# A two-layer attention and mixture kernel on one core: the contexts of eight heads as one step or as two

## The reference, cut to what matters

```
gate_v = _get_sel_gate(x, sel_v_w, rs)      # top 2 of 8 experts per head
gate_o = _get_sel_gate(x, sel_o_w, rs)
xv  = einsum('bsd,hedp->bshep', x, v_w)     # 64 products of 128x128 per batch
v   = einsum('bshep,bshe->bhsp', xv, gate_v)
att = softmax(einsum('bhqp,bhkp->bhqk', q, k) * SCALE, axis=-1)
ctx = einsum('bhqk,bhkp->bqhp', att, v)     # the contexts
out = einsum('bshep,hepd->bsd', ctx[:, :, :, None, :] * gate_o[..., None], o_w)
```

## Time and profile before

| what | us |
|---|---|
| median of 3 runs | 1510.36 |
| the profiled execution, whole | 1512.08 |
| its span, first to last instruction | 1509.9 |
| PE busy | 1439.0 |
| DVE busy | 1320.1 |
| ACT busy | 1274.5 |
| POOL busy | 861.5 |
| PE idle in the first 160 us | 51.6 |
| mean granted TensorE clock over the span | 0.975 |

### The profile page before, as it was taken

One profiled execution on the slowest core, in us unless ns is written; L12 is line 12 of the kernel. 1 busy time (PEld: TensorE's weight loads), 2 busy tenths in 40 slices (PEclk: granted clock), 3 DMA queues, 4 the chain that ended last, 5 costly groups with the idle time before them and its releaser, 6 DMA issues.

```text
span 1509.9 us, 34239 instructions
## 1 busy us (share of the span) xinstructions
PE 1439.0 (95%) x9905; PEld 971.3 (64%) x9905; DVE 1320.1 (87%) x4496; ACT 1274.5 (84%) x4428; POOL 861.5 (57%) x1345
## 2 busy tenths in 40 slices
PE   3678999999999999999999999999999999999997
PEld 2355666666666666666666666666666666666654
DVE  3767988999999999999999999999999999999886
ACT  3667888899888888988888898888889988888886
POOL 2112666565565656556565665656566565655567
PEclk8588999999999999999999999999999999999999
DMA  4510000000000000000000000000000000000000
GB/s 126 148 46 17 13 16 15 14 13 14 12 14 14 16 14 13 14 12 15 13 16 14 13 14 12 14 14 16 14 13 13 12 16 13 16 11 6 7 3 4
DMA packets 68954, 30.13 MB, mean 20 GB/s; under 512 B 19168, under 2 KB 68768, under 8 KB 68768
## 3 DMA queue, kind: packets, MB, share of 16 engines
q1 hardware_dynamic: 51552, 19.31, 4.8%
q10 hardware_dynamic: 17216, 8.65, 2.0%
HBM read 17.31 MB, written 2.10 MB: 13 GB/s over the span
## 4 chain that ended last, share of the span: by engine, by line
PE 86%; POOL 4%; DVE 4%; issue 2%; ACT 2%; DMA 1%; SPq 1%; POOLq 0%; ACTq 0%; DVEq 0%
PE psC L307 55%; PE psA L307 14%; PE psB L307 7%; PE psB L530 3%; PE psC L626 2%; POOL accO L3426 2%; POOL TE L3414 1%; PE psA L463 1%; PE psB L550 1%; DVE TE L2487 1%; PE psA L419 1%; POOL v_sb L3419 1%; DVE PTB L2350 1%; PE psC L572 1%; DVE nmA L2226 1%
## 5 line engine op out<-in xcount | busy, mean ns | idle before, releaser
L3426 POOL TENSOR_TENSOR accO<-accO,TE 128x512 f32<-128x512 f32 x192 | 246.7, 1285 | 140.8 <-DVE TE L2487 133.9
L2487 DVE SCALAR_TENSOR_TENSOR TE<-psC,gateO,TE 128x128 f32<-128x128 f32 x1024 | 287.5, 343 | 32.5 <-ACT TE L1334 23.6
L1334 ACT ACTIVATE TE<-psC,gate 128x128 f32<-128x128 f32 x1024 | 303.4, 420 | 9.5 <-PE psC L307 8.1
L2487 DVE SCALAR_TENSOR_TENSOR TE<-psC,gate,TE 128x128 f32<-128x128 f32 x1024 | 287.8, 343 | 25.9 <-PE psC L307 19.3
L1334 ACT ACTIVATE TE<-psC,gateO 128x128 f32<-128x128 f32 x1024 | 289.3, 380 | 20.1 <-PE psC L307 11.9
L3414 POOL TENSOR_TENSOR TE<-TE 128x256 f32<-128x256 f32 x256 | 189.3, 739 | 166.0 <-DVE TE L2487 159.5
L307 PE MATMUL psC<-Vh,xTh 128*128 128x512 f32 x512 | 266.1, 520 | 1.9 <-DVE TE L2487 0.6
L307 PE MATMUL psC<-Oh,ch 128*128 128x512 f32 x512 | 266.1, 520 | 1.1 <-DVE cl L2479 0.9
L307 PE MATMUL psC<-Oh,cl 128*128 128x512 f32 x512 | 202.5, 396 | 0.0
L307 PE MATMUL psC<-Vh,xTl 128*128 128x512 f32 x512 | 202.3, 395 | 0.0
L307 PE MATMUL psC<-Vl,xTb 128*128 128x512 bf16 x512 | 199.7, 390 | 0.0
(11 more groups left out here) (226 smaller groups left out, 3445.5 us busy)
## 6 DMA issues: line engine op xcount, KB each, us to landing
bdB<-Kc SPq DMA_DIRECT2D x384, 16.0 KB
raw<-in_L_ffn_v_w ACTq DMA_DIRECT2D x8, 512.0 KB, 4.3
raw<-in_L_ffn_o_w ACTq DMA_DIRECT2D x8, 512.0 KB, 4.1
x_sb<-in_x SPq DMA_DIRECT2D x32, 64.0 KB, 1.8
ctx_sb<-in_ctx SPq DMA_DIRECT2D x32, 64.0 KB, 2.0
Qb<-Qc SPq DMA_DIRECT2D x128, 8.0 KB
bdA<-Kc SPq DMA_DIRECT2D x128, 8.0 KB
bias_sb<-in_mask_Bx1xSxS_ff SPq DMA_DIRECT2D x32, 64.0 KB, 1.9
```

Of the source, the lines that this page charges most:

```text
L1334: return A.activation(o, i, func, **kw)
L2487: m = V.scalar_tensor_tensor(TE[:, i, e], psC[:, p, e * P:(e + 1) * P], gates[:, e:e + 1], TE[:, i, e], ALU.mult, ALU.add)
L3426: G.tensor_tensor(accO[:], TE[:, slot(b, H1)] if h == 1 else accO[:], TE[:, slot(b, H1 + h)], ALU.add).then_inc(o_fe, 1)
```

## The change

c_context of PE is split in two: c_context(b, 0) computes heads 0 to 3 in the first half of a pair of banks, c_context(b, 1) heads 4 to 7 in the second half of another pair. A batch therefore takes 22 pairs. In the round, c_context(i - 4, 0) stands between values 5 and values 6, and c_context(i - 4, 1) between outputs 0 and outputs 1. In the last batches the first stands after values 5 or 6 and the second after outputs 1 or 2. The steps of ACT and DVE read the new places, and stand in their lists accordingly. All five engines' lists are written anew, in start, period and end: on PE the b_ and a_ steps between the values and outputs move by a place or two; on DVE the round is cut at another point, and some steps (c_weights, b_keys, the statistics) move; on SP the loop is cut one round later, and in start the mask's load stands ahead of that of k_w; POOL's second gate product goes after outputs 6. No arithmetic is added or taken away. The core of the diff:

```diff
-            def c_context(b):
-                if b not in BATCHES:
-                    return
-                ps, free = pair(("c", b))
-                for h in range(H1):
-                    if h % 4 == 0:
-                        pe.wait_ge(*free[h // 4])
-                        pe.wait_ge(c_pt, 2 * b + h // 4 + 1)
+
+            def c_context(b, i):
+                if b not in BATCHES:
+                    return
+                ps, free = pair(("c", b, i))
+                pe.wait_ge(*free[i])
+                pe.wait_ge(c_pt, 2 * b + i + 1)
+                for h in range(4 * i, 4 * i + 4):
                     pe.wait_ge(v_fe, 2 * (H1 * b + h + 1))
                     m = mm(ps[:, h * P:(h + 1) * P], v_sb[:, h], PTC[:, h])
-                    if h % 4 == 3:
-                        m.then_inc(c_ctx, 1)
-                        free[h // 4] = (c_cl, 2 * b + h // 4 + 1)
+                m.then_inc(c_ctx, 1)
+                free[i] = (c_cl, 2 * b + i + 1)
 
             def outputs(b, h, half):
                 if b not in BATCHES:
...
                 a_proj(i - 1)
                 values(i - 4, 4, 1)
                 values(i - 4, 4, 0)
+                b_att(i - 2)
                 values(i - 4, 5, 1)
-                b_att(i - 2)
                 values(i - 4, 5, 0)
+                b_keys(i - 1)
+                c_context(i - 4, 0)
                 values(i - 4, 6, 1)
-                b_keys(i - 1)
+                values(i - 4, 6, 0)
                 b_proj(i - 2)
-                values(i - 4, 6, 0)
                 values(i - 4, 7, 1)
+                values(i - 4, 7, 0)
+                b_values(i - 1)
                 a_x1t(i - 1)
-                values(i - 4, 7, 0)
+                outputs(i - 4, 0, 1)
                 a_route(i - 1)
-                c_context(i - 4)
                 a_shared(i - 1)
-                outputs(i - 4, 0, 1)
                 outputs(i - 4, 0, 0)
+                c_context(i - 4, 1)
+                outputs(i - 4, 1, 1)
                 a_ht(i - 1)
-                b_values(i - 1)
-                outputs(i - 4, 1, 1)
+                outputs(i - 4, 1, 0)
                 a_ffn(i - 1)
-                outputs(i - 4, 1, 0)
+                outputs(i - 4, 2, 1)
                 a_ctxt(i)
-                outputs(i - 4, 2, 1)
                 outputs(i - 4, 2, 0)
                 a_xt(i)
                 a_keys(i)
                 outputs(i - 4, 3, 1)
+                a_values(i)
+                a_queries(i)
+                outputs(i - 4, 3, 0)
                 b_xt(i - 1)
-                outputs(i - 4, 3, 0)
                 outputs(i - 4, 4, 1)
                 outputs(i - 4, 4, 0)
                 b_queries(i - 1)
-                a_queries(i)
-                a_values(i)
                 outputs(i - 4, 5, 1)
+                outputs(i - 4, 5, 0)
...
-                copy(four(ch, i), psC[:, place["c", b], 512 * i:512 * i + 512]).then_inc(c_ch, 1)
+                copy(four(ch, i), psC[:, place["c", b, i], 512 * i:512 * i + 512]).then_inc(c_ch, 1)
                 b_att(i - 2)
                 values(i - 4, 5)
                 b_keys(i - 1)
+                c_context(i - 4, 0)
                 values(i - 4, 6)
+                c_short(i - 4, 0)
+                values(i - 4, 7)
                 a_x1t(i - 1)
-                values(i - 4, 7)
-                c_context(i - 4, 0)
+                outputs(i - 4, 0)
                 a_gap(i - 1)
-                c_short(i - 4, 0)
+                b_values(i - 1)
+                a_shared(i - 1, 0)
+                a_shared(i - 1, 1)
                 c_context(i - 4, 1)
-                a_shared(i - 1, 0)
+                a_ht(i - 1)
                 c_short(i - 4, 1)
-                a_shared(i - 1, 1)
-                a_ht(i - 1)
-                outputs(i - 4, 0)
                 outputs(i - 4, 1)
-                b_values(i - 1)
                 a_ctxt(i)
+                a_xt(i)
+                a_keys(i)
                 outputs(i - 4, 2)
-                a_keys(i)
+                a_values(i)
+                a_queries(i)
...
-                V.tensor_tensor(four(cl, i), psC[:, place["c", b], 512 * i:512 * i + 512], f(four(ch, i)),
+                V.tensor_tensor(four(cl, i), psC[:, place["c", b, i], 512 * i:512 * i + 512], f(four(ch, i)),
                 c_choice(i - 3, 7)
+                c_choice(i - 3, 8)
+                c_choice(i - 3, 9)
                 a_attend(i - 1, 0)
                 a_attend(i - 1, 1)
-                c_choice(i - 3, 8)
-                c_choice(i - 3, 9)
-                c_weights(i - 3, 0)
-                values(i - 4, 2)
                 c_choice(i - 3, 10)
                 b_attend(i - 2, 0)
+                b_attend(i - 2, 1)
+                values(i - 4, 2)
                 values(i - 4, 3)
                 a_first(i - 1, 0)
-                b_attend(i - 2, 1)
                 values(i - 4, 4)
                 a_first(i - 1, 1)
                 a_stats2(i - 1, 0)
+                values(i - 4, 5)
                 a_stats2(i - 1, 1)
+                b_keys(i - 1)
                 a_stats2(i - 1, 2)
-                values(i - 4, 5)
+                c_context(i - 4, 0)
+                values(i - 4, 6)
                 a_norm2(i - 1)
-                values(i - 4, 6)
+                c_weights(i - 3, 0)
                 values(i - 4, 7)
-                b_keys(i - 1)
                 b_third(i - 2)
+                a_stats(i, 0)
                 a_top(i - 1, 0)
+                a_stats(i, 1)
+                a_top(i - 1, 1)
+                a_top(i - 1, 2)
                 c_stats(i - 2, 0)
-                a_top(i - 1, 1)
-                a_stats(i, 0)
-                a_top(i - 1, 2)
-                a_stats(i, 1)
                 c_stats(i - 2, 1)
-                c_context(i - 4, 0)
+                a_routed(i - 1, 0)
                 c_stats(i - 2, 2)
-                a_routed(i - 1, 0)
+                a_routed(i - 1, 1)
                 a_stats(i, 2)
+                a_routed(i - 1, 2)
+                outputs(i - 4, 0)
+                c_choice(i - 3, 11)
+                a_norm(i)
+                c_share(i - 3, 0)
+                c_norm(i - 2)
+                c_share(i - 3, 1)
+                c_context(i - 4, 1)
+                c_share(i - 3, 2)
+                c_share(i - 3, 3)
+                a_second(i - 1)
+                c_share(i - 3, 4)
+                b_stats(i - 1, 0)
+                b_stats(i - 1, 1)
+                c_share(i - 3, 5)
+                b_stats(i - 1, 2)
+                outputs(i - 4, 1)
+                b_norm(i - 1)
+                outputs(i - 4, 2)
...
                 weights_switch()
                 products()
+                masks(0)
                 products2()
-                masks(0)
                 a_queries(0)
                 a_masks(0)
                 a_keys(0)
+                inputs(1)
...
             def period(i):
-                masks(i)
-                bias(i - 1)
-                inputs(i)
+                inputs(i - 1)
+                masks(i - 1)
+                b_keys(i - 3)
+                a_keys(i - 2)
+                a_queries(i - 2)
                 a_masks(i - 1)
-                b_keys(i - 2)
-                a_keys(i - 1)
-                a_queries(i - 1)
-                store(i - 5)
+                bias(i - 2)
+                store(i - 6)
...
                 values(B - 1, 5, 1)
                 values(B - 1, 5, 0)
+                c_context(B - 1, 0)
                 values(B - 1, 6, 1)
                 values(B - 1, 6, 0)
                 values(B - 1, 7, 1)
                 values(B - 1, 7, 0)
-                c_context(B - 1)
                 outputs(B - 1, 0, 1)
                 outputs(B - 1, 0, 0)
                 outputs(B - 1, 1, 1)
                 outputs(B - 1, 1, 0)
                 outputs(B - 1, 2, 1)
                 outputs(B - 1, 2, 0)
+                c_context(B - 1, 1)
                 outputs(B - 1, 3, 1)
...
```

More of the change, by code:

```diff
@@ L691, in start @@
                 a_scores(0, 1)
+                b_keys(0)
                 a_scores(0, 2)
@@ L1003, in start @@
                 values(2, 6, 0)
-                b_values(5)
-                values(2, 7, 1)
-                a_x1t(5)
-                values(2, 7, 0)
-                a_route(5)
-                c_context(2)
-                a_shared(5)
-                outputs(2, 0, 1)
-                outputs(2, 0, 0)
+                c_context(2, 0)
+                values(2, 7, 1)
+                values(2, 7, 0)
+                b_keys(5)
+                a_x1t(5)
+                outputs(2, 0, 1)
+                a_route(5)
+                a_shared(5)
+                outputs(2, 0, 0)
+                c_context(2, 1)
+                b_values(5)
                 a_ht(5)
@@ L1689, in start @@
                 b_att(0)
+                cut(13)
                 b_keys(1)
@@ L2524, in start @@
                 a_maxt(0, 0)
```

(53 more changed lines are left out.)

1354 lines of the change are left out of this document (652 added, 702 removed).

## The result

The changed kernel takes 1499.94 us (median of 4, 1497.01 to 1502.12), the kernel before 1510.64 us in the same rounds (4, 1509.99 to 1511.52). The ratio is 0.9928, 95% interval 0.9910 to 0.9946: 10.7 us faster. The prediction said 1499.3. The sum was right to 0.4 us of gain, and several of its terms were not; that is what most of the following is about.

What follows compares the result with a forecast made beforehand. Taken as bounds: wait chains in the front, PE's pace in the steady part, an end with open waits. Terms -5.6 - 0 - 1.1 - 4.4 - 0 = -11.1 us took 1510.4 to 1499.3; range 1490 to 1512.

Steps and rivals of the forecast that it cites:

- The bubble: Steady round, eight context products: PE waits for v_sb of head 7, 0.30 us per round hidden in its busy time.
- The steady rounds: Contexts of batches 1 to 28: 0.20 us gained per round, 5.6 us in all, bounds 0.8 and 8.4.
- What comes instead: Steady rounds: expert products broken up at three more places, costing 0.1 us per round.
- the bubble only moves: Steady part: PE waits for ACT or DVE instead, 0 gained there; 1504.9 us in all, chance 0.18.
- The places in psC: Values 6 and outputs 1, on pairs used one head back: nothing lost, at most 0.55 us per round.
- The rival's price: Late drain before second halves of values 6 and outputs 1: up to 0.55 us per round, 1514.7 us, chance 0.16.
- Batch 0: Between its context and first output: waiting for v_sb, ch and cl removed, 1.1 us gained.
- End: Last three batches: v_sb waits, output gaps and POOL's later start removed, 4.4 us gained, bounds 2.5 and 6.
- the 0.3 us of gap per batch: Last three batches: gap in the outputs while cl and gateO are made, 0.30 us each, 0.9 gained.
- the 0.3 for POOL: Kernel end: POOL's adds start sooner and its small backlog goes, 0.3 us gained.
- Front: Start stage, up to 160 us: new start sequences taken as 0, between 5 us gained and 5 lost.
- The mask's chain: Start stage: mask load no longer behind that of k_w, on the chain to the first scores, up to 1.65 us.

Runs made afterwards that it cites:

- h9: Kernel before, with one unread 128x128 add on POOL ahead of v_sb of head 7 in each batch: 1521.92 us.
- h10: Changed kernel, with one unread 128x128 add on POOL ahead of v_sb of head 7 in each batch: 1503.16 us.
- h1: Kernel before with its own lists, only the context split and its PE, ACT and DVE steps moved: 1612.54 us.
- the second profile: Changed kernel run again with nothing altered; median 1502.12 us, profiled execution 1501.55 us.
- the first profile: First profiled execution of the changed kernel, nothing else altered: 1497.01 us.
- h5: Kernel before, with SP issuing the mask row of batch 0 ahead of k_w: 1508.56 us.
- h6: Changed kernel, with SP issuing the mask row of batch 0 behind the loads for products, as before: 1505.36 us.

## Why the prediction was right, and where it was not

The total was right (1499.3 against 1499.94) and so were the sign and the mechanism of the steady rounds and of the end. But about half of the gain came from the start, which the prediction had left at nothing. Point by point:

- **The bubble: right, and confirmed.** A busy share of 99.5% hid a wait for v_sb of head 7. h9 lengthens it by 0.41 us and the round by 0.37; h10, with the split, lets the same delay pass. I had put it at 0.30, against a product of 0.224, and that is what the undisturbed sets of the changed kernel show: 0.90 us for four, 1.79 for eight against 2.09.
- **The steady rounds: 0.20 us each predicted, 0.142 found (43.94 to 43.80), 3.4 us for 4.8 in the 24 rounds from c_xt(4) to c_xt(28).** The failed term is "What comes instead". It held only the broken rows of expert products, 0.1, and they cost nothing: the four contexts between two expert halves took 0.90 us, which is 4 x 0.224. Of the 0.30 regained, 0.16 are missing. 0.12 of these are the new bubble at outputs 4 behind b_xt, for ACT, which I had not seen coming; c_xt's wait of 0.21 for DVE costs nothing in the balance. The last 0.04 are open. So the rival "the bubble only moves" held for two fifths of it.
- **The places in psC: right for the changed lists, by little.** There is no wait at values 6 or outputs 1. The rival's price was too low: with DVE's and ACT's lists left as they were, PE loses 3.35 us in a round (h1), 1.50 of them in this wait, where 0.55 was the bound. I had bounded DVE's part only; ACT drains the other half, and it was ACT that outputs 1 waited for.
- **Batch 0: 1.1 us predicted.** The wait of 0.86 us for cl is gone. It lies in the piece from values(0, 2, 1) to values(1, 2, 1), which is 1.7 us shorter as a whole; in the pieces after it, up to c_xt(4), 1.3 are lost again, and the prediction has no term for that. No run tells which moves bring the one or the other.
- **End: 4.4 us predicted, 1.2 to 1.8 found from c_xt(28) on, where the 0.4 of batches 27 and 28 belong too.** The failed step is the sum of gaps as if each were a gain. The waits for v_sb went (2.4 us; I had counted 3.2), POOL's idle time fell as said, but the 0.3 us of gap per batch and the 0.3 for POOL did not add to that. A longer wait for DVE's TE (0.8 for 0.6, 1.3 in the second profile) and others of 0.4 (xTl, PTB) took part of it back, and on the way out of the rounds, from c_xt(28) to values(28, 2, 1), the changed kernel is 0.6 us slower (58.11 for 57.48).
- **Front: 0 predicted, 5.6 found before values(0, 2, 1).** That is more than the bound of 5 on either side; the first profile even has 9.1 there. The mask's chain was found and priced at up to 1.65 us, then left out against "a hundred small moves". It was worth 2.65 (h5) to 3.2 (h6). The other 2.4 to 3.0 us stay open: the new start lists and the granted clock, which differs from one execution to the next, were not told apart. It exceeded my price because a load issued sooner also landed in less: the mask was issued 1.7 us sooner, and the first scores started 4.3 us sooner, since the copies into bdA no longer ran beside the two 512 KB loads of v_w that ACT issues at 21.5 us. That their company made them slow is read from the order of the transfers, not shown by a run of its own.

So 10.7 = 6.1 + 3.4 + 1.2 (to c_xt(4), to c_xt(28), to the end) stood against 11.1 = 1.5 + 4.8 + 4.8. The first was 4.6 us too low, the others 1.4 and 3.6 too high. That the total came out within 0.4 us is luck. The steady term, whose cause h9 and h10 prove, was right in its cause and too high by 0.06 in 0.20 per round.

## What to carry to other kernels

Where an in-order engine seems full, compare start-to-start distances of like instructions: the one that is longer than its kind shows a wait, and a small delay added to its producer shows whether it counts. The price of a group of products is read from the distance between like products around it, not from its start to that of the next, other product. Splitting a step changes the drain distances of a rotation of buffers, so the lists of all engines that drain have to be moved with it; the split alone cost 101 us here. Where two orders are compared piece by piece, the marks must be such that the same work lies before them. In a start-up stage, look first at the order of DMA issues on the chain to the first product, and fill TensorE's gaps if its granted clock is at the lower level.

## What the runs showed of the hardware that I had not expected

- The same kernel has a front that differs from run to run by 3.5 us and then repeats to 0.01 us over 1186 us (c_xt(1) to c_xt(28)). The granted clock between 60 and 90 us was 0.80 in one execution and 0.63 in the other; h6, without any added matmul, had 1.00 from 30 to 80 us in its profile.
- The clock can fall in the steady part as well. In h1, where PE stands still for 0.94 and 1.50 us in a round, the granted clock from 730 to 750 us was 0.91, and an expert matmul's record at 739 us was 0.63 us long for 0.40 elsewhere. It falls in some rounds only: the mean from 400 to 1200 us was 0.99, for 1.00 in the kernel before.

```profile
700.00:730.00 30.00, 29.79 (x233) 20.41 (x230) 27.48 (x86) 28.12 (x101) 17.68 (x28) 1.00 0.05 12
730.00:750.00 20.00, 17.56 (x87) 11.20 (x86) 14.86 (x60) 12.44 (x45) 10.61 (x17) 0.91 0.05 14
```

- 63 matmuls whose output nobody reads made the kernel 5.7 us faster, at a granted clock of 0.98 for 0.63 from 60 to 90 us.
